# A four-layer gated cross-attention model on one core: the last two attentions by heads of 64, and two roundings moved to ScalarE

## What is computed

```python
q = (x @ Wq).reshape(b, n, HEADS, DIM_HEAD)          # 8 heads of 64
k = (context @ Wk).reshape(b, m, HEADS, DIM_HEAD)
v = (context @ Wv).reshape(b, m, HEADS, DIM_HEAD)
attn = softmax(einsum('bihd,bjhd->bhij', q, k) * SCALE)
out = einsum('bhij,bjhd->bihd', attn, v).reshape(b, n, HEADS * DIM_HEAD)
return out @ Wout + bout

def act_quant(x):
    scale = 127.0 / clip(max(abs(x), axis=-1), EPS, None)
    return clip(round(x * scale), -128.0, 127.0) / scale
def bitlinear(x, w): return act_quant(x) @ weight_quant(w).T
g = bitlinear(x, w_gate); u = bitlinear(x, w_up)
return bitlinear(square(relu(g)) * u, w_down)

x = x + tanh(g_xattn[2]) * xattn2(layernorm(x), ctx); x = x + tanh(g_ffn[2]) * ffn2(layernorm(x))
x = x + tanh(g_xattn[3]) * xattn3(layernorm(x), ctx); x = x + tanh(g_ffn[3]) * ffn3(layernorm(x))
```

## Time and profile before

| | before |
|---|---|
| median of 3 runs | 1649.75 us (1649.02 to 1652.42) |
| profiled execution: time | 1648.05 us |
| profiled execution: span | 1646.3 us |
| TensorE busy (matmul) | 1494.6 us, 91% |
| VectorE busy | 1190.2 us, 72% |
| ScalarE busy | 874.5 us, 53% |
| GpSimd busy | 582.6 us, 35% |
| mean granted TensorE clock | 0.934 |

### The profile page before, as it was taken

One profiled execution on the slowest core, in us unless ns is written; L12 is line 12 of the kernel. 1 busy time (PEld: TensorE's weight loads), 2 busy tenths in 40 slices (PEclk: granted clock), 3 DMA queues, 4 the chain that ended last, 5 costly groups with the idle time before them and its releaser, 6 DMA issues.

```text
span 1646.3 us, 43347 instructions
## 1 busy us (share of the span) xinstructions
PE 1494.6 (91%) x14329; PEld 1046.6 (64%) x14329; DVE 1190.2 (72%) x4951; ACT 874.5 (53%) x1741; POOL 582.6 (35%) x1120
## 2 busy tenths in 40 slices
PE   6999999988998779898889689989988999899998
PEld 5888888875665445454477456656655665566665
DVE  6777877766777799999837744436888888865554
ACT  5656666654554555555323255555566666655543
POOL 4455544540000666666136411103322232222221
PEclk9999999998999687888669889999999999999999
DMA  8000000006200000000010000000000000000000
GB/s 191 2 0 0 0 0 0 0 2 138 52 0 14 1 0 0 0 0 0 2 46 0 15 19 0 0 0 2 1 2 0 0 1 1 2 8 7 6 13 20
DMA packets 40363, 22.41 MB, mean 14 GB/s; under 512 B 23231, under 2 KB 37790, under 8 KB 40158
## 3 DMA queue, kind: packets, MB, share of 16 engines
q1 hardware_dynamic: 40286, 21.42, 5.5%
HBM read 17.22 MB, written 4.19 MB: 13 GB/s over the span
## 4 chain that ended last, share of the span: by engine, by line
PE 63%; DVE 21%; issue 8%; ACT 4%; POOL 2%; DVEq 1%; DMA 0%; POOLq 0%; ACTq 0%
PE ps L681 7%; PE ps L690 7%; PE ps L2099 5%; PE ps L2094 5%; DVE arena L1355 5%; DVE arena L1349 4%; PE ps L303 3%; PE ps L310 3%; PE ps L352 3%; PE ps L332 3%; PE ps L2149 3%; PE ps L2160 2%; PE ps L343 2%; PE ps L323 2%; PE ps L2138 2%
## 5 line engine op out<-in xcount | busy, mean ns | idle before, releaser
L2262 ACT COPY arena<-ps 128x512 f32<-128x512 f32 x128 | 75.1, 587 | 150.9 <-PE ps L2099 150.9
L2094 PE MATMUL ps<-arena 128*128 128x128 f32 x1024 | 138.2, 281 | 3.4 <-ACT arena L2299 3.4
L681 PE MATMUL ps<-xnT,arena 128*128 128x512 f32 x256 | 135.1, 621 | 0.0
L2099 PE MATMUL ps<-arena 128*64 128x512 f32 x512 | 135.0, 605 | 0.0
L2094 PEld LDWEIGHTS ps<-arena 128*128 128x128 f32 x1024 | 126.8, 196 | 4.9 <-ACT arena L2299 4.4
L2557 POOL TENSOR_TENSOR arena<-arena 128x512 f32<-128x512 f32 x64 | 67.9, 1061 | 130.5 <-DVE arena L2493 130.0
L574 POOL TENSOR_TENSOR ln_veps<-ln_mv,eps 128x4 f32<-128x4 f32 x40 | 10.8, 269 | 269.0 <-DVE ln_mv L568 269.0
L1813 DVE TENSOR_SCALAR_CACHE_REDUCE thr_hits<-thr_abs,thr_candidate 128x512 bf16<-128x512 f32 (+1 forms) x248 | 101.8, 477 | 0.0
L1355 DVE MATCH_REPLACE8 arena<-arena 128x64 f32<-128x64 f32 x512 | 101.7, 210 | 0.1
L830 DVE SCALAR_TENSOR_TENSOR x_res<-ps,arena,x_res 128x128 f32 (+1 forms) x256 | 72.0, 345 | 31.1 <-PE ps L690 28.5
L2256 ACT COPY arena<-ps 128x512 f32<-128x512 f32 x128 | 77.1, 605 | 29.2 <-PE ps L2094 28.8
(11 more groups left out here) (409 smaller groups left out, 3978.4 us busy)
## 6 DMA issues: line engine op xcount, KB each, us to landing
toeplitz<-ssm_toeplitz_scratch SPq DMA_DIRECT2D x2, 2048.0 KB, 18.1
ssm_toeplitz_scratch<-ssm_padded_kernel SPq DMA_DIRECT2D x1, 2048.0 KB, 11.3
out<-x_res SPq DMA_DIRECT2D x8, 256.0 KB, 2.3
arena<-ctx SPq DMA_DIRECT2D x2, 768.0 KB, 6.0
arena<-L_ffn_W SPq DMA_DIRECT2D x2, 512.0 KB
arena<-L_xattn_Wq SPq DMA_DIRECT2D x1, 512.0 KB, 6.2
x_res<-x SPq DMA_DIRECT2D x1, 512.0 KB, 7.6
arena<-L_xattn_Wo SPq DMA_DIRECT2D x1, 512.0 KB, 8.2
```

Source lines behind the costliest of these rows:

```text
L681: nc.tensor.matmul(ps[:, u % 3, :], w1[:, x, c * P:(c + 1) * P], xnT, start=True, stop=True).then_inc(h_full.sem, 1)
L2094: last = T_.matmul(ps[:, 1 - n, j * P:(j + 1) * P], folded[phase].mT[:, 4 * n + j, :], cg[:, s, :], start=True, stop=True)
L2099: last = T_.matmul(ps[64 * m:64 * m + 64, 4, :], cg[:, s, b * CTX:(b + 1) * CTX], folded[phase].wvo[:, m, :, :], start=True, stop=True)
L2262: S.copy(VW[:, r % 2, b, :, :].rearrange("p c d -> p (c d)"), ps[:, 4, :]).then_inc(v_laid.sem, 1)
```

## The change

- `fold_weights` goes. `attention_weights` only loads the weights of layers 2 and 3 (14 DMAs instead of 10, all behind the last part of the convolution), Wo in two copies with the halves of its 128-row blocks swapped in the second. `gate_weights` scales Wo and bo by the gate on ScalarE before the decoder.
- A round forms queries (4 products of 128x128) and keys (4 of 96x128), scores as 16 products of 64x64 (8 heads, 2 sequences), values as 4 of 256 columns, heads (probabilities by values) as 16 of 64x64, and y = heads by Wo (8 of 128 columns). ScalarE copies queries, keys, values and heads, once each. KT, QT, PT and OT have one buffer each where G and PT had two.
- The bias is added to x by GpSimd. y goes to bank 0 of PSUM, and scores to banks 3 and 4.
- `hq = h * sh + ROUND` and the same for the four quantized tiles (`qf`) go to ScalarE; VectorE keeps the subtraction and the clip (`clip_h`, `clip_q`), which stand behind the scores' subtraction now. The exp moves ahead of the relu, the adding of y behind the clip, and the adding of feed-forward 2's result behind h's maximum.

```diff
-        k.fold_pool(e)
...
-        k.fold_act(e)
...
-        k.fold_pe(e)
...
+def attention_weights(k, io, name, wq, wk, wv, wo, bo, inputs, outputs, conv_part):
...
+    w.q, w.k, w.v, w.bo = inputs.f32(INNER), inputs.f32(INNER), inputs.f32(INNER), inputs.f32(D)
+    w.o = outputs.f32(2, C, D)
...
-    G = cv.f32(2, heads, P)
-    VW = cv.f32(2, 2, C, D)
-    PR = cv.f32(2, heads, CTX)
-    PT = cv.f32(2, C, P)
+    KT, QT = cv.f32(C, P), cv.f32(C, P)
+    VH = cv.f32(2, 2, C, 64)
+    PR = cv.f32(2, C, 2, CTX)
+    PT = cv.f32(C, P)
+    OT = cv.f32(2, C, SEQ)
...
+    def queries(e, t, s, phase):
+        e.wait_ge(xt_laid.sem, xt_laid.at(t + 1))
+        for c in range(C):
+            last = T_.matmul(ps[:, 1, c * P:(c + 1) * P], weights[phase].q[:, c * P:(c + 1) * P], xnT[:, s * P:(s + 1) * P], start=True, stop=True)
+        last.then_inc(q_full.sem, 1)
...
+    def quarters():
+        return [(c, b, m, slice(64 * m, 64 * m + 64), slice(64 * b, 64 * b + 64)) for c in range(C) for b in range(2) for m in range(2)]
...
     def pe_step(e, t, r, b):
...
+            e.wait_ge(v_laid.sem, v_laid.at(t - 1))
+            e.wait_ge(q_laid.sem, q_laid.at(t + 1 if r < STEPS else STEPS))
+            e.nop(nofuse=True)
+            for c, b_, m, rows, toks in quarters():
+                out = slice(64 * (m ^ b_), 64 * (m ^ b_) + 64)
+                last = T_.matmul(ps[out, 1 + b_, c * SEQ:(c + 1) * SEQ], VH[rows, s, b_, c, :], PT[rows, c, toks], start=True, stop=True)
+            last.then_inc(o_full.sem, 1)
+        if attend(r):
+            e.wait_ge(k_laid.sem, k_laid.at(t + 1))
+            e.wait_ge(q_laid.sem, q_laid.at(t + 1))
+            e.wait_ge(s_sub.sem, s_sub.at(t))
+            e.nop(nofuse=True)
+            for c, b_, m, rows, toks in quarters():
+                last = T_.matmul(ps[toks, 3 + m, c * CTX:(c + 1) * CTX], QT[rows, c, toks], KT[rows, c, toks], start=True, stop=True)
+            last.then_inc(s_full.sem, 1)
+            e.wait_ge(c_laid.sem, c_laid.at(t + 1))
+            e.wait_ge(v_laid.sem, v_laid.at(t))
+            values(e, s, phase)
+        if 2 <= r < STEPS + 2:
+            e.wait_ge(o_laid.sem, o_laid.at(t - 1))
...
             for c in range(C):
                 for m in range(2):
-                    last = T_.matmul(ps[64 * m:64 * m + 64, 5, 0:D], PT[:, s, c, 64 * m:64 * m + 64], VW[:, s, m, c, :],
-                                     start=(c == 0), stop=(c == C - 1))
+                    last = T_.matmul(ps[64 * m:64 * m + 64, 0, 0:D], OT[:, m, c, :], w_o[:, m, c, :], start=(c == 0), stop=(c == C - 1))
             last.then_inc(y_full.sem, 1)
...
+        if ahead(r, 1):
+            e.wait_ge(s_sub.sem, s_sub.at(t + 1))
+            turn_xn(e, t + 1, o)
...
+        if 2 <= r < STEPS + 2:
+            e.wait_ge(x_done.sem, x_done.at(t - 1))
...
     def act_step(e, t, r, b):
         s, o = r % 2, 1 - r % 2
+        if downs(r):
+            e.wait_ge(a_recip.sem, a_recip.at(t - F2))
+            e.wait_ge(hq_done.sem, hq_done.at(t - F2 - 1))
+            S.activation(hq[:], h[:], ACT.Identity, bias=magic[:, 0:1], scale=sh[:, 0:1]).then_inc(hr_done.sem, 1)
+        if 2 <= r < STEPS + 2:
+            copy_heads(e, t)
         if attend(r):
...
+        if norms(r, 2) and r < LN3:
+            g = b - 2
+            e.wait_ge(q_step.sem, q_step.at(4 * g + 3))
+            for j in range(GT):
+                last = S.activation(qf[:, j, :], k.xn[:, 0, j, :], ACT.Identity, bias=magic[:, 0:1], scale=sc[:, j:j + 1])
+            last.then_inc(q_step.sem, 1)
...
-        e.wait_ge(a_recip.sem, a_recip.at(n))
-        V.tensor_scalar(hq[:], h[:], sh[:, 0:1], ROUND, ALU.mult, ALU.add).then_inc(hr_done.sem, 1)
+
+    def clip_h(e, t):
...
+            xb = k.x[:, tile_of(t, r), :]
+            G_.tensor_tensor(xb, xb, weights[r // TILES].bo, ALU.add).then_inc(x_biased.sem, 1)
```

More of the change, by code:

```diff
@@ L1972, in decoder @@
+        halves = io[wo].rearrange("(c m p) d -> m p c d", m=2, p=half)
+        for m in range(2):
+            e.dma_start(w.o[half * m:half * m + half, 1, :, :], halves[1 - m]).then_inc(w.loaded.sem, 16)
+    return dict(sp=sp), w
+def decoder(k, io, weights, freed):
     nc, ps = k.nc, k.ps
@@ L2231, in pe_step @@
                 last.then_inc(o3_full.sem, 1)
[L2232 to L2237 removed]
     def pe(e):
+        for w in weights:
+            e.wait_ge(w.loaded.sem, w.loaded.at(w.count))
+            e.wait_ge(w_gated.sem, w_gated.at(4))
         e.wait_ge(before.sem, before.end)
[L2241 to L2243 removed]
+        keys(e, 0, 0, 0)
         turn_xn(e, 0, 0)
[L2245 to L2246 removed]
+        queries(e, 0, 0, 0)
         steps(e, lambda t, r, b: pe_step(e, t, r, b))
```

309 lines of the change are left out of this document (123 added, 186 removed).

## The result

| | before | with the change |
|---|---|---|
| median of 4 runs each, same chip | 1651.09 us (1649.02 to 1652.65) | 1633.79 us (1629.28 to 1634.59) |
| ratio | | 0.989 (95% interval 0.987 to 0.991) |
| profiled execution: time, span | 1648.05, 1646.3 us | 1629.28, 1627.5 us |
| busy TensorE, VectorE, ScalarE, GpSimd | 1494.6, 1190.2, 874.5, 582.6 us | 1460.4, 1175.5, 909.0, 607.7 us |

A forecast was written before the change was run, and what follows sets the result against it. Folding lay alone on the path; TensorE bound rounds 41 to 62, VectorE set the long rounds of 10 to 40. Terms -6.8 - 2 - 12 - 16 = -36.8 us led to 1612 us, range 1582 to 1638.

The forecast's parts named there:

- Rounds 0 to 9, -2: Decoder's first rounds: copies show, so a third of TensorE's 0.72 us a round is left: -2 us, ends 0 and -7.
- Rounds 10 to 40, -12: Decoder rounds with the quantized feed-forward: a group of four falls from 32.2 to 30.6 us, -12 us in all.
- The loop: Rounds 10 to 40: chain from VectorE's 1/scale of h through ScalarE, TensorE, ScalarE and VectorE, 7.25 us a round.
- the leg from y to the relu: TensorE's part of the 7.25 us chain in rounds 10 to 40: y, xn's transpose, gate and landing, 1.45 us.
- Rounds 41 to 62, -16: Decoder rounds with feed-forward 3: TensorE stays the bound and 22 rounds gain 0.72 us each, -16 us.
- The end, 0: The last rounds after 63 stay as they were: 0 us.
- Folding, -6.8: Layer 1: without the folding, POOL's rstd ends at 850.3 and the first hidden product starts at 853.1, not 859.9: -6.8 us.
- TensorE's round, -0.72: Each decoder round: y, values, heads and scores take 2.98 us instead of 3.71, -0.72 us; ends -0.8 and 0.
- the rival of 0.01: All 64 decoder rounds: the 64x64 products do not run side by side, +2.5 us a round, 1772 us; chance 0.01.
- ScalarE's queue as the bound of every round: All decoder rounds: rounding and copies in ScalarE's queue set the pace, +35 us, 1685 us; chance 0.08.
- Rounds 10 to 40 gain nothing: In these decoder rounds TensorE's saved time turns into waits for ScalarE; -25 us in all, 1625 us; chance 0.25.
- The open loop: Rounds 10 to 40: the chain is looser than drawn, rounds go to 6.5 us, kernel 1575 us; chance 0.13.

The follow-up runs named there:

- experiment 7: Kernel with heads copied before h is rounded, plus exp's table loaded before the decoder: 1608.34 us; plus unread TensorE products around the decoder's start: 1605.49 us.
- experiments 1 and 3: First: changed kernel, heads copied before h is rounded, 1610.25 us. Third: h rounded twice, in the changed kernel 1661.47 us, in the first's kernel 1619.01 us.
- experiment 2: Changed kernel with TensorE issuing the quantized feed-forward's gate and up products before y instead of after: 1631.83 us.
- experiment 8: 20 unread TensorE products where the folding used to run, added to the last kernel of experiment 7: 1603.64 us, against 1606.30 without them.
- experiment 5: Kernel before the change, still folded: rounding on ScalarE with the new order, 1685.76 us; h rounded behind the values' copies, 1678.71; new order alone, 1673.60.
- heads-first kernel: Changed kernel with ScalarE copying the heads out of PSUM before it rounds h, instead of after: 1610.25 us, ratio 0.976.

## Why the prediction was wrong

It had the direction, and twice the gain: 37 us forecast, 17 measured. That 1633.79 us lies inside the range of 1582 to 1638 confirms nothing: the upper end was there for slower mechanisms than the ones in the sum, and five terms of the sum missed on the same side, rounds 0 to 9 by 7.9 us, rounds 10 to 40 by 5.6, rounds 41 to 62 by 3.0, the end by 2.6 and the folding by 1.9. The 3.5 us by which code that the change doesn't touch was faster in the profiled execution hide a part of that. By the prediction's own terms:

- **Rounds 0 to 9, -2, measured +5.9.** The worst term, outside its ends of 0 and -7. The price was taken from rows at full clock. I saw that copies would show here, but not that the gaps between the first products, and products that no longer stand back to back, would keep the clock down for two rounds. With the gaps filled the ten rounds take 67.3 us (experiment 7): the clock is 5.1 us of the miss, the table's load 0.7, and the gain of 2 is not there even at full clock.
- **Rounds 10 to 40, -12, measured -6.4.** The loop was the right one (experiments 1 and 3). The step that failed is the leg from y to the relu: it was drawn through the gate product, and goes through the copy of xn (experiment 2), 1.69 us instead of 1.45. The other three legs are within 0.05 us in a loop that nothing else cuts into (7.53 us in all, 7.25 forecast). My allowance for the group's extras, 1.6 us, was too large by 0.5 (31.22 - 4 x 7.53 = 1.1), though it left out one that is there: in one round of four ScalarE's rounding of q, not VectorE's scale, is what the next rounding of h waits for. The two errors partly cancel: 0.6 us a group, 5 us of the stage. The price of the rounding was entered as 0.6 us, though the text takes the square's 0.68; it is 0.72 to the next start. A gain that is the small difference of two large sums needs its legs better than this.
- **Rounds 41 to 62, -16, measured -13.0.** TensorE stayed the bound. The steady rounds gave 0.70 us each (7.98 to 7.28 on average). What lacks is in the rounds that turn x (7.7 to 7.9 us instead of 8.4, so 0.5 to 0.7) and above all in the first two, 18.6 us after 18.3 before, where the quantized feed-forward's last steps still queue: with the heads first they take 17.0. The term multiplied all 22 rounds by the gain of a steady one.
- **The end, 0, measured +2.6.** Simply not followed: "the last rounds after 63 stay". In them heads have no scores and values behind them to cover their copy.
- **Folding, -6.8, measured -4.9.** The place and what is late next were right. The step that failed is that POOL's rstd "now ends at 850.3": it took POOL's sums from rows where VectorE stood idle. Beside VectorE's own sums they last longer, and rstd ended 1.4 us later than this (7.45 us behind the copy instead of 6.1). The other 0.6 us is TensorE, whose transposes were priced from a row behind the folding's own products and run at the lower clock without them (experiment 8: 0.5 us up to the first hidden product; its other 1.7 us lie in the next stretch).
- **TensorE's round, -0.72.** Right: 3.02 us for 2.98. The 64x64 products run side by side (the rival of 0.01 falls), and the change of shape is inside the sum: the outs take 0.99 us ahead of the heads where the keys take 0.89 ahead of the outs, and the steady round still gives 0.70. The Trainium skill (TensorEngine Tiling (Array Packing), Key Properties) says that changing the tiling mode drains TensorE. These 0.1 us may be that drain, which no run here shows by itself; the 10 us that the estimate by it added did not come.
- **The rivals.** ScalarE's queue as the bound of every round did not come. What experiment 5 shows is its place, not its load: in the folded kernel the rounding ahead of the copies of values lost 15.8 us in this stage (of 36.5, the others are the order's), with ScalarE busy for 191 of 286 us. "Rounds 10 to 40 gain nothing" was nearest, at 1625, and its mechanism is there in part: of the 16 us that TensorE saved in this stage, 9.6 turned into waits, and it gained 6. The open loop is what the heads-first kernel comes to in part: 222.9 us, where I had put 6.5 us a round, 201.
- **The sum.** -36.8 us from the median of 1649.75 gives 1613.0, not 1612, and the four legs add up to 7.27, not 7.25. Neither matters here.

## What to carry to other kernels

Before moving work to a less busy engine, look at which instruction of its queue it will stand ahead of: against the same kernel with the rounding on VectorE, it was worth nothing ahead of the heads' copy and 20 us behind it, and adding another one cost 25 us in one place and 9 in the other, though the engine was busy for only four fifths of the time. Price what you remove with its neighbours: products that go away can take TensorE's clock along for what follows, and work that they kept apart can meet, as GpSimd's and VectorE's sums did here. And where one chain closes through four engines, follow each leg through the queues as written, not through the data alone; filling an engine's idle time inside the loop gained nothing.
